# Perceiver block on one core: four down-weight buffers, a peeled last turn with the last two items summed by TensorE, and an index bound on gather and scatter

## What is computed

```python
xn = _layernorm(x)
top_w, top_i = lax.top_k(softmax(xn @ gate_w.T), 6)          # 32 experts, 6 for each token
h = silu(xb @ w1[e]) * (xb @ w3[e])                          # xb: the rows of expert e, 512 -> 352
ob = h @ w2[e]                                               # 352 -> 512
y = zeros.at[token].add(ob * weight)
shared = (silu(xn @ sw1) * (xn @ sw3)) @ sw2
x = x + y + shared
```

## Time and profile before

| | us |
|---|---|
| median of 3 runs | 1063.48 |
| lowest and highest | 1063.03, 1066.78 |
| the profiled execution | 1069.81 |
| its span | 1068.0 |
| of that, items on PE, first up product to end of the last down product | 756.1 to 1049.5 |
| from there to the end of the span | 18.5 |

### The profile page before, as it was taken

The page is one execution under the profiler, slowest core; times in us unless marked ns, Lnnn a source line. Parts: engine busy times, 40 slices in busy tenths (PEclk is TensorE's granted clock), DMA queues, the critical chain, the costliest instruction groups (busy, mean ns, idle before and its releaser), DMA issues.

```text
span 1068.0 us, 18826 instructions
## 1 busy us (share of the span) xinstructions
PE 986.1 (92%) x5428; PEld 824.3 (77%) x5429; DVE 666.2 (62%) x994; ACT 543.1 (51%) x888; POOL 272.0 (25%) x188
## 2 busy tenths in 40 slices
PE   6999899999999869999999998799998999998792
PEld 5788699898998748888888886588776776776681
DVE  5645665667656557777777875557466666666563
ACT  5444666665666545555555525332454554554451
POOL 2200122121221133333222414200132232232222
PEclk9899999999999999999999999899999999999997
DMA  9000452332125041222112024106489999999986
GB/s 314 31 0 1 107 183 81 98 98 76 45 76 130 1 148 60 79 66 70 59 60 98 20 104 159 59 1 255 147 255 276 297 276 352 336 292 279 316 238 184
DMA packets 76059, 152.92 MB, mean 143 GB/s; under 512 B 11264, under 2 KB 38272, under 8 KB 75776
## 3 DMA queue, kind: packets, MB, share of 16 engines
q1 hardware_dynamic: 67728, 132.92, 37.1%
q0 software_dynamic: 8304, 19.67, 8.6%
HBM read 153.87 MB, written 14.55 MB: 158 GB/s over the span
## 4 chain that ended last, share of the span: by engine, by line
PE 63%; issue 12%; SPq 11%; DVE 4%; DMA 4%; ACT 3%; POOL 2%; ACTq 0%; DVEq 0%; POOLq 0%
PE ps L311 15%; PE ps L312 15%; PE ps L313 15%; SPq L847 6%; PE ps L672 6%; PE ps L876 4%; DMA w_raw<-in_w 2%; SPq L1010 2%; POOL wo_l L451 1%; SPq L1013 1%; SPq L1014 1%; PE ps L731 1%; PE ps L738 1%; PE ps L748 1%; PE ps L659 1%
## 5 line engine op out<-in xcount | busy, mean ns | idle before, releaser
L876 PE MATMUL ps<-w_raw,hT 128*128 (+3 forms) x264 | 124.3, 607 | 20.2 <-DMA w_raw<-in_w 17.8
L892 DVE TENSOR_TENSOR w_l<-w_raw,w_h 128x1408 fp32r<-128x1408 f32 x78 | 124.8, 1639 | 21.9 <-issue 13.2
L888 ACT ACTIVATE w_h<-w_raw 128x1408 fp32r (+1 forms) x78 | 103.3, 1369 | 25.1 <-issue 16.0
L694 POOL TENSOR_TENSOR lw_l<-lw_raw,lw_h 128x1024 fp32r<-128x1024 f32 x32 | 77.0, 2409 | 146.6 <-ACT lw_h L690 146.1
L985 POOL DMA_INDIRECT xe<-xn_scratch,take x39 | 39.2, 1004 | 259.1 <-DVE ob L956 173.2
L876 PEld LDWEIGHTS ps<-w_raw,hT 128*128 128x128 f32 (+1 forms) x264 | 48.0, 191 | 68.0 <-issue 67.7
L311 PE MATMUL ps<-w_h,xeT_h 128*128 x288 | 96.6, 335 | 1.6 <-DVE w_l L892 1.6
L313 PE MATMUL ps<-w_h,xeT_l 128*128 x288 | 93.4, 324 | 0.0
L312 PE MATMUL ps<-w_l,xeT_h 128*128 x288 | 92.9, 323 | 0.0
L311 PE MATMUL ps<-xT_hi,lw_h 128*128 128x512 f32 x192 | 77.3, 402 | 0.0
L312 PE MATMUL ps<-xT_lo,lw_h 128*128 128x512 f32 x192 | 76.5, 398 | 0.0
(11 more groups left out here) (297 smaller groups left out, 2610.4 us busy)
## 6 DMA issues: line engine op xcount, KB each, us to landing
w_raw<-in_w SPq DMA_DIRECT2D x86, 704.0 KB
w_raw<-in_w SPq DMA_DIRECT2D x40, 512.0 KB
w_raw<-in_w SPq DMA_DIRECT2D x40, 192.0 KB
rkB<-rk_scratch SPq DMA_DIRECT2D x56, 128.0 KB, 3.2
wq_raw<-in_Wq SPq DMA_DIRECT2D x8, 512.0 KB, 4.7
wo_raw<-in_Wo SPq DMA_DIRECT2D x16, 256.0 KB, 2.9
lw_raw<-in_kwT SPq DMA_DIRECT2D x8, 512.0 KB, 3.4
lw_raw<-in_qwT SPq DMA_DIRECT2D x8, 512.0 KB, 3.3
```

The lines of the kernel that those rows point to most:

```text
L694: e.tensor_tensor(lw_l[n][:, :, :], lw_raw[n][:, :, :], lw_h[n][:, :, :], ALU.subtract).then_inc(lw_ready[n], 1)
L876: m = e.matmul(ps[:, 6 + k, :], hT[r, k, c, :], w2_raw[r, slot(w), c, :], start=c == 0, stop=c == FC - 1)
L888: e.activation(w13_h[:, k, n, :, :], w13_raw[:, slot(raw), n, :, :], ACT.Copy).then_inc(w13_hi_s, 1)
L892: e.tensor_tensor(w13_l[:, k, n, :, :], w13_raw[:, slot(raw), n, :, :], w13_h[:, k, n, :, :], ALU.subtract).then_inc(w13_ready, 1)
```

## The change

- **w2 buffers:** four instead of two, with the buffer chosen by a new row `FIRST` of the table (the number of the expert's first item, modulo 4). w1 and w3 use the same row. The two new buffers lie in memory that held routing lists (`seat`, `item`), so their first loads wait until PE has read these (`PS_TOKENS`).
- **A row `HELD`** says how many items later a buffer comes free because of a repeat. `ODD` and `HIGH` go out of SP's waits.
- **SP's order:** w2 of items 1, 2 and 3 is issued in a row behind w1 and w3 of item 4; from then on w2 is issued for item m+4 beside w1 and w3 for item m+5. The loop ends at item 36 and 35. Both kinds of load read four values of the table for an item, where they read three.
- **The last turn is peeled** on every engine; no gather, split or scatter for items behind the end.
- **The last two items** go to their tokens by TensorE: DVE builds two 0/1 matrices `home` (128 x 512, from an iota and the token list), PE multiplies them with the two `ob` tiles into four PSUM banks (eight matmuls), DVE adds them to x.
- **Read back:** each scratch in one transfer, behind a wait for all weight loads (`past_loads`, formerly at the very end) and for the scatters of the items before the last two. DVE adds both only after its last `ex_dve_ob`.
- **Index bound** T - 1 on gather and scatter: a padding seat moves no row. `xe` is cleared once.

```diff
-        w2_raw = sbuf(moe, "w2_raw", [P, 2, FC, D])
+        w2_raw = w2_and_lists[:, 0:4 * W2].rearrange("p (w c d) -> p w c d", w=4, c=FC)
+        y_back = [xn_c, w2_and_lists[:, 4 * W2:4 * W2 + TT * D].rearrange("p (t d) -> p t d", t=TT)]
...
-        def raw_slot(e, m, k):
-            if isinstance(m, int):
-                return m % 4
-            return item_value(e, HIGH, m) * 2 + k
+        def raw_slot(e, m):
+            return item_value(e, FIRST, m, 3)
...
         def ex_load_w13(e, m, k, before):
-            ex, new, raw = item_value(e, EXPERT, m, E - 1), item_value(e, LOADED, m), raw_slot(e, m, k)
+            ex, new = item_value(e, EXPERT, m, E - 1), item_value(e, LOADED, m)
+            static = isinstance(m, int) and m < 4
+            raw, held = (m, 0) if static else (raw_slot(e, m), item_value(e, HELD, m, 3))
             for n, w in enumerate((w1_r, w3_r)):
-                if not isinstance(m, int) or m >= 2:
+                if not static:
+                    e.wait_ge(w13_ready, m * 2 + (held * 2 + (n - 3)))
+                    e.sem_inc(acc_turn, 1)
+                elif m >= 2:
                     e.wait_ge(w13_ready, m * 2 + (n - 3))
                 e.wait_ge(w13_in[k][n], before * 16)
-        def ex_load_w2(e, m, k):
+        def ex_load_w2(e, m, k, before):
             ex, new = item_value(e, EXPERT, m, E - 1), item_value(e, LOADED, m)
-            if isinstance(m, int) and m == 0:
-                e.wait_ge(d_ps, TT)
+            w = m if isinstance(m, int) and m < 4 else raw_slot(e, m)
+            if isinstance(m, int) and m < 2:
+                e.wait_ge(d_ps, TT * (m + 1))
+            elif isinstance(m, int) and m < 4:
+                e.wait_ge(small_ps, PS_TOKENS)
             else:
-                e.wait_ge(d_ps, m + item_value(e, ODD, m) + (NSH - 1))
+                e.wait_ge(d_ps, m + item_value(e, HELD, m, 3) + (NSH - 3))
+                e.sem_inc(acc_turn, 1)
+            e.wait_ge(w2_in[k], before * 32)
...
-            ex_load_w2(e, 1, 1)
+            for m in (1, 2, 3):
+                ex_load_w2(e, m, m % 2, m // 2 + 1)
             for m in range(2):
                 ex_load_w13(e, m + 5, 1 - m, m + 3)
-                ex_load_w2(e, m + 2, m)
-            with e.Fori(1, last_i + 1) as i:
+                ex_load_w2(e, m + 4, m, 3)
+            with e.Fori(1, last_i - 1) as i:
                 for k in range(2):
                     ex_load_w13(e, i * 2 + (k + 5), 1 - k, i + (k + 3))
-                    ex_load_w2(e, i * 2 + (k + 2), k)
-            e.wait_ge(acc_done[0], last_i * 16 + 16)
+                    ex_load_w2(e, i * 2 + (k + 4), k, i + 3)
+            e.wait_ge(past_loads, 6)
+            e.wait_ge(acc_done[0], last_i * 16)
...
+                                 bounds_check=T - 1, oob_is_err=False).then_inc(xe_in[k], 16)
...
+                e.tensor_scalar(home[:, k, :], iota_t[:, :], tl_f[:, 1, bass.ds(last_i * 2 + k, 1)], None,
+                                ALU.is_equal).then_inc(home_ready, 1)
...
+                e.tensor_tensor(x[:, t, :], x[:, t, :], ps[:, t, :], ALU.add).then_inc(out_ready, 1)
...
+            def to_tokens(k, t):
+                return e.matmul(ps[:, t, :], home[:, k, t * P:(t + 1) * P], ob[:, k, :], start=k == 0, stop=k == 1)
```

More of the change, by code:

```diff
@@ L237, in perceiver_block @@
         w13_l = sbuf(moe, "w13_l", [P, 2, 2, DC, FF], F32R)
[L238 removed]
+        W2 = FC * D
+        SEATS = TT * TOP_K * P
+        w2_and_lists = sbuf(moe, "w2_and_lists", [P, 2 * W2 + TT * TOP_K * (P + 2 * ML)])
+        w2_raw = w2_and_lists[:, 0:4 * W2].rearrange("p (w c d) -> p w c d", w=4, c=FC)
+        seat = w2_and_lists[:, 2 * W2:2 * W2 + SEATS].rearrange("p (q n) -> p q n", n=P)
+        item = w2_and_lists[:, 2 * W2 + SEATS:].rearrange("p (q a n) -> p q a n", a=2, n=ML)
+        y_back = [xn_c, w2_and_lists[:, 4 * W2:4 * W2 + TT * D].rearrange("p (t d) -> p t d", t=TT)]
         moe.close()
@@ L295, in perceiver_block @@
         acc_done = [sem("acc_done0"), sem("acc_done1")]
-        y0_in, y1_in = sem("y0_in"), [sem(f"y1_in{t}") for t in range(TT)]
-        y_sum, out_ready = sem("y_sum"), sem("out_ready")
+        y0_in, y1_in = sem("y0_in"), sem("y1_in")
+        y_sum, out_ready, home_ready, last_ps = sem("y_sum"), sem("out_ready"), sem("home_ready"), sem("last_ps")
         w13_in = [[sem(f"w{1 + 2 * n}_in{k}") for n in range(2)] for k in range(2)]
@@ L922, in ex_pe_xT, with ex_pe, ex_act @@
             last.then_inc(xeT_ps, 1)
-        def ex_pe(e, i, k, first=False):
+        def ex_pe(e, i, k, first=False, last=False):
             m = i * 2 + k
             e.wait_ge(xeT_ready, m + 1)
-            ex_pe_xT(e, 1 - k, i + (k + 1))
+            if not last:
+                ex_pe_xT(e, 1 - k, i + (k + 1))
             e.wait_ge(h_ready, m + (NSH - 1))
             ex_up(lambda c: xeT_h[:, k, c, :], lambda c: xeT_l[:, k, c, :], k, item_value(e, SLOT, m), m * 2 + 6)
-            ex_down(e, 1 - k, m + (NSH - 1), 1 if first else item_value(e, SLOT, m - 1),
+            ex_down(e, 1 - k, m + (NSH - 1), 1 if first else item_value(e, FIRST, m - 1, 3),
                     (w2_in[1], 32) if first else (w2_in[1 - k], i * 32 + (k + 1) * 32), m + (NSH - 2))
             ex_hT(e, k, m + NSH)
-        def ex_act(e, i, k):
+        def ex_act(e, i, k, last=False):
             m = i * 2 + k
+            ex_act_hT(e, 1 - k, m + (NSH - 1))
+            if last:
+                ex_act_silu(e, k, m + NSH)
+                return
             odd = item_value(e, ODD, m + 1)
-            ex_act_hT(e, 1 - k, m + (NSH - 1))
+            raw = None if isinstance(m, int) and m == 0 else raw_slot(e, m + 1)
             ex_act_xT(e, m + 1, 1 - k)
@@ L963, in ex_dve_x, with ex_dve @@
             e.tensor_tensor(x[:, u % TT, :], x[:, u % TT, :], ps[:, 6 + u % 2, :], ALU.add).then_inc(d_read, 1)
-        def ex_dve(e, i, k):
+        def ex_dve(e, i, k, ahead=None, last=False):
             m = i * 2 + k
+            if last:
+                ex_dve_ob(e, ahead, k)
+                ex_dve_h(e, k, m + NSH)
+                return
             ex_dve_xT(e, m + 1, 1 - k)
@@ L1380, in _ @@
             ex_act(e, 0, 1)
-            with e.Fori(1, last_act + 1) as i:
+            with e.Fori(1, last_act) as i:
                 ex_act(e, i, 0)
                 ex_act(e, i, 1)
+            ex_act(e, last_act, 0)
+            ex_act(e, last_act, 1, last=True)
             ex_act_hT(e, 1, last_act * 2 + (NSH + 1))
@@ L1808, in _ @@
             ex_pe(e, 0, 1)
-            with e.Fori(1, last_i + 1) as i:
+            with e.Fori(1, last_i) as i:
                 ex_pe(e, i, 0)
                 ex_pe(e, i, 1)
-            ex_down(e, 1, last_i * 2 + (NSH + 1), item_value(e, SLOT, last_i * 2 + 1), (w2_in[1], last_i * 32 + 64),
-                    last_i * 2 + NSH)
+            ex_pe(e, last_i, 0)
+            ex_pe(e, last_i, 1, last=True)
+            def to_tokens(k, t):
+                return e.matmul(ps[:, t, :], home[:, k, t * P:(t + 1) * P], ob[:, k, :], start=k == 0, stop=k == 1)
+            e.wait_ge(home_ready, 2)
+            e.wait_ge(d_read, last_i * 2 + (NSH + 1))
+            to_tokens(0, 0)
+            ex_down(e, 1, last_i * 2 + (NSH + 1), item_value(e, FIRST, last_i * 2 + 1, 3), (w2_in[1], last_i * 32 + 64),
+                    last_i * 2 + NSH)
+            for t in range(1, TT):
+                to_tokens(0, t)
+            e.wait_ge(d_read, last_i * 2 + (NSH + 2))
+            for t in range(TT):
+                to_tokens(1, t).then_inc(last_ps, 1)
 def kernel(x, ctx_1024, L0_xattn_Wq, L0_xattn_Wk, L0_xattn_Wv, L0_xattn_Wo, L0_xattn_gq, L0_xattn_gk,
```

131 lines of the change are left out of this document (72 added, 59 removed).

## The result

The changed kernel takes 1078.14 us (median of 4 runs, 1077.21 to 1081.68) where the kernel before takes 1065.13 (4 runs): ratio 1.013, 95% interval 1.009 to 1.016. A second measurement gave 1.013 again (E5). The interval leaves out 1, so it is slower, by 1.3%, and 3 us beyond the top of the predicted range. Its profiled execution took 1078.14 us too, with a span of 1076.4.

The account below looks back on a forecast made before the run. SP's instruction stream was taken as the bound: at 8.7 us an item the last down product ends at 1053.5, plus a 13.4 tail gives span 1066.9 against 1068.0; -1.1 from 1063.48 gives 1062 us, range 1046 to 1075.

Parts of the forecast that it names:

- What bounds the kernel now: MoE stage: SP's own instructions for issuing transfers, 7.63 us an item against PE's 7.39, not mainly the two w2 buffers.
- SP's stream: SP's instructions in the item loop: value loads +1.08, w2 +0.28, w1 and w3 +0.07, together +1.43 us an item.
- P = 8.7: SP's pace in us an item after the change, hold-ups partly included; 8.4 to 9.1 kept, all above PE's 7.39.
- SP's start: First loads on SP before the loop's steady pace: w2 of item 5 issued near 785.3, item 35 then at 1046.3.
- Landing: Last w2 load, from its first transfer's issue to arrival: 4.2 us, with up to 7.7.
- The tail: From the last down product's end to the span's end: 13.4 us instead of 18.5, a saving of 5.1.
- Padding as slack: Gather and scatter: a third fewer rows, some 31 us of DMA time, save no time while SP is the bound.
- the slow one: Rival on SP's pace: hold-ups stay at their mean, 9.05 us an item, 1073 to 1076 us; chance 0.22.
- The cheap stream: Rival on SP's pace: hold-ups vanish or value loads overlap better, 8.4 us an item, 1053 us; chance 0.27.
- Buffers win: Rival: SP much quicker in timed runs, PE the bound, 17.8 us of waits go, 1038 us; chance 0.10.
- The Trainium skill's floor of about 600 ns for a tensor_load: Rival on SP's value loads: at 0.60 us each, 9.36 us an item and 1082 us; chance 0.03.
- w2 starts 8.5 to 9 us apart: Sign in the profile after: spacing of SP's w2 transfer starts from item 10 on; 7.5 or less would refute the argument.

Follow-up runs that it names:

- E5: The changed kernel again with no edit, beside the kernel before: 1078.86 us, ratio 1.013.
- E1: Changed kernel with w2 issued right behind its item's w1 and w3 from one set of value loads, 4 an item, not 8: 1042.97 us, ratio 0.973.
- E9: E1 unchanged, four value loads an item, run again in the third set: 1041.49 us, ratio 0.970.
- E11: E1 with 4 unused value loads more an item, eight in all: 1089.33 us, ratio 1.016.
- E6: Kernel before, still two w2 buffers, with 3 value loads an item in place of 6: 1062.50 us, ratio 0.998.
- E4: Kernel before with the index bound alone and xe cleared once: 1070.16 us against 1070.82, ratio 1.000.
- E3: Changed kernel without the index bound on gather and scatter: 1093.76 us, ratio 1.022.
- E2: Kernel before with two unused value loads more an item on SP: 1104.83 us against 1070.82, ratio 1.032.
- E10: E1 with 2 unused value loads more an item, six in all: 1057.95 us, ratio 0.986.
- E8: E1 with DVE adding the first scratch between its last two ob: 1040.17 us, ratio 0.976.
- E12: E6 with the index bound on gather and scatter: 1062.33 us against 1071.96 for the kernel before, ratio 0.991.
- E7: E1 without the index bound on gather and scatter: 1044.26 us, ratio 0.982.

## Why the prediction was wrong

Forecast 1062, range 1046 to 1075, measured 1078. The mechanism was the one forecast, a term of the sum was too small, and with it went the sign. By its own steps:

- **What bounds the kernel now:** right for the changed kernel (E1, E9 to E11). For the kernel before, 7.63 us against PE's 7.39 holds only with the hold-ups of its trace; undisturbed it is 7.11. And the two buffers, set aside because SP waited so rarely, were the next limit (E6): SP did not wait for them only because it was late itself.
- **SP's stream, +1.43 us an item: this is the step that failed.** The undisturbed streams are 7.11 and 8.82, so the change added 1.70. By lines, value loads took 1.17 more for the 1.08 in the sum, w2's addresses and waits 0.33 for 0.28, and w1's and w3's 0.21 for 0.07: their waits now have register arithmetic, a separate instruction each and semaphore increments. 30 x 0.27 = 8 us.
- **P = 8.7:** 0.3 too low, 9 us, and nearly all of it is that term. It holds 7.1 + 1.43 and leaves 0.17 for hold-ups; the changed kernel's trace has 0.18. So to take less than the mean hold-up was right, by luck: the reasons given for it, fewer bytes and the recording, are not what the traces show. And that 7.63 + 1.43 = 9.06 comes so near the measured 9.00 is two errors that cancel, hold-ups that did not come and instructions that did.
- **SP's start:** w2 of item 5 was put at 785.3 and came at 785.03. With the measured 9.00 it gives 1055.3 for item 35; it was 1054.98.
- **Landing:** 4.2 us taken, 5.5 measured (1054.98 to 1060.5), inside its upper bound of 7.7. (The product's start, put at 1050.7, is 1050.5 by its own terms.)
- **Not in the sum:** the last down product ran 4.53 us, not 2.84. PE had idled 1.51 us before it, and the granted clock is 0.64 over that stretch (below), between the levels of 1.2 and 2.4 GHz. 1.7 us.
- **The tail:** 13.4 us predicted, 11.2 measured. The first scratch was there when DVE was (1066.11, 5.5 us behind its issue) because the slow last product gave it time. The saving is 7.3 us, not 5.1.
- **Sum of the differences:** +8.7 for the issue of the last w2, +1.3, +1.7, -2.2 gives +9.5 on a span of 1066.9: 1076.4, the measured span.
- **From the span to the time:** the other 6.3 us of the miss. The difference of two spans was taken off 1063.48, the median of the timed runs, while the profiled execution of before took 1069.81 and that of the changed kernel just its median, 1078.14. The first has the hold-ups and the second has not; timed runs of before without them would fit the 6.3 us, and the 1064.93 of the second set.
- **Padding as slack:** right in the kernel before (E4, 1.000). In the changed kernel no run settles it (E3).
- **The rivals:** the slow one, at a chance of 0.22, had the right P (9.05) for the wrong reason: the hold-ups did not stay at their mean. The cheap stream's condition, hold-ups that vanish, nearly came, and P was 9.0 and not 8.4. "Buffers win" had a time (1038) that takes a lighter stream as well (E1). The Trainium skill's floor of about 600 ns for a tensor_load ("DMA: Bandwidth & Descriptors", section "Latency and other measured facts") doesn't hold for these, whose median is 0.27 us: in E11 four more cost 2.34 us, 0.58 each with their register work.

Of what was to show it, this came: w2 starts 8.5 to 9 us apart (9.0), hardly a wait of SP for PE, waits of PE before up products (18 of them, so in half of the items and not in most), DMA share near 0.85 (0.86 and 0.78). The tail was not near 13 us, and DVE did not wait for a scratch. PE in the windows view of the changed kernel, the last row over its last down product (busy us of PE, PEld, DVE, ACT, POOL with their instructions, then granted clock, DMA share and GB/s):

```profile
860.00:960.00 100.00, 87.14 (x407) 68.94 (x407) 57.12 (x78) 46.24 (x67) 29.05 (x22) 0.95 0.86 270
960.00:1060.00 100.00, 86.10 (x401) 66.66 (x401) 55.93 (x77) 43.69 (x66) 26.89 (x20) 0.97 0.78 240
...
1060.50:1065.30 4.80, 4.61 (x7) 2.01 (x8) 0.00 (x0) 0.00 (x0) 0.00 (x0) 0.64 0.65 215
```

And the same first stretch in E1:

```profile
860.00:960.00 100.00, 96.92 (x481) 74.78 (x480) 66.72 (x92) 55.11 (x78) 35.70 (x26) 1.00 0.98 318
```

In the two stretches in which late loads make PE idle the granted clock is 0.95 and 0.97, in E1 it is 1.00: the waits go with a little clock lost on top.

## What to carry to other kernels

Add up the instructions of the engine that issues the transfers, with their register work, for one turn of the loop, and compare that with one turn of the busiest engine: a buffer more that costs two value loads an item can take away more than it gives. Count the small ones too, a wait with register arithmetic and an increment; here they were most of the miss. When two limits lie close together, lift both or neither: the whole change with eight value loads an item cost 1.3%, three in place of six in the kernel before gave 0.2% (E6), and the change with four gave 3% (E1), of which some 0.7% is its shorter tail. And before two traces are compared, look whether their instructions have the same longest times: a median of many turns separates what an edit adds from what the execution adds.

## What the runs showed of the hardware

- "PE waits for DMA" was issue time: two unused value loads an item on SP turned 17.8 us of such waits into 42.2 (E2).
- One value load more an item, with its register work, adds 0.47 to 0.55 us to SP's undisturbed stream (E2, E10, E11); the load alone has a median of 0.27.
- SP's instructions of any kind are held up by about 0.7 us now and then in some traces and never in others, 0.5 to 0.9 us an item and none, for the same stream (E1 and E9 against E8, E12 against E6). They do not follow the traffic: E7 has none at a DMA share of 1.01 and E4 0.50 with the padding rows left out.
- PE's granted clock in the changed kernel, by stretches of 20 us: 0.91 to 0.94 in five between 880 and 1040, in all of which PE waited for late loads; others with as much waiting have 1.00. In E1 it is 1.00 from 740 to 1032.
